# A bank of its own for the sums of r in a GRU with a mixture of experts behind it; shared banks for units and expert blocks

## The reference

```python
def cell(h, x):
    gi = x @ W_ih + b_ih
    gh = h @ W_hh + b_hh
    i_r, i_z, i_n = jnp.split(gi, 3, axis=-1)
    h_r, h_z, h_n = jnp.split(gh, 3, axis=-1)
    r = jax.nn.sigmoid(i_r + h_r)
    z = jax.nn.sigmoid(i_z + h_z)
    n = jnp.tanh(i_n + r * h_n)
    h_new = (1.0 - z) * n + z * h
    return (h_new, h_new)
...
gu = jnp.einsum('th,ehf->etf', x, w_gate_up)
act = _silu_and_mul(gu)
eo = jnp.einsum('eti,eih->eth', act, w_down)
routed = jnp.einsum('te,eth->th', combine, eo)
shared = _silu_and_mul(x @ w_sh_gate_up) @ w_sh_down
```

## Time and profile before

| | us |
|---|---|
| median of 3 runs | 1204.74 (1201.41 to 1206.31) |
| the profiled execution | 1195.19 |
| its span | 1193.4 |
| TensorE (PE) busy | 1036.9 (87%), 13452 products |
| VectorE (DVE) busy | 850.0 (71%) |
| ScalarE (ACT) busy | 573.3 (48%) |
| GpSimd (POOL) busy | 206.2 (17%) |

### The profile page before, as it was taken

One profiled execution on the slowest core, in us unless ns is written; L12 is line 12 of the kernel. 1 busy time (PEld: TensorE's weight loads), 2 busy tenths in 40 slices (PEclk: granted clock), 3 DMA queues, 4 the chain that ended last, 5 costly groups with the idle time before them and its releaser, 6 DMA issues.

```text
span 1193.4 us, 35909 instructions
## 1 busy us (share of the span) xinstructions
PE 1036.9 (87%) x13452; PEld 623.1 (52%) x13452; DVE 850.0 (71%) x4089; ACT 573.3 (48%) x1877; POOL 206.2 (17%) x213
## 2 busy tenths in 40 slices
PE   2789888889999898999899989998998898889894
PEld 2556555556665454555455545554555454555452
DVE  5898999868889888677867787678787778721111
ACT  4755555655555543445344434443444444435442
POOL 0200011020110212111211121112120112233332
PEclk9999999999999999999999999999999999999897
DMA  8943455381864753623451234234342144488694
GB/s 307 402 147 97 144 180 186 107 205 56 294 237 173 197 193 73 230 75 61 125 178 29 55 101 166 56 55 174 129 126 55 28 143 134 121 296 278 181 288 56
DMA packets 68829, 183.13 MB, mean 153 GB/s; under 512 B 7737, under 2 KB 40288, under 8 KB 61344
## 3 DMA queue, kind: packets, MB, share of 16 engines
q1 hardware_dynamic: 45632, 107.74, 25.5%
q0 software_dynamic: 23024, 73.11, 23.1%
HBM read 137.01 MB, written 52.87 MB: 159 GB/s over the span
## 4 chain that ended last, share of the span: by engine, by line
PE 51%; DVE 27%; ACT 10%; issue 7%; DMA 3%; POOL 0%; POOLq 0%; SPq 0%; ACTq 0%; DVEq 0%
PE psG L715 17%; PE psG L721 14%; PE psU L778 6%; DVE arena L1046 5%; DVE arena L1044 5%; ACT arena L1429 4%; ACT arena L1425 4%; PE psS L824 3%; DVE arena L1054 3%; DVE arena L1069 3%; DVE arena L1065 3%; DVE arena L1056 3%; PE psD L790 3%; DVE arena L1048 2%; PE psO L845 2%
## 5 line engine op out<-in xcount | busy, mean ns | idle before, releaser
L715 PE MATMUL psG<-arena 128*32 128x384 f16 x4096 | 213.8, 329 | 76.1 <-DVE arena L1069 68.2
L1425 ACT ACTIVATE arena<-arena 128x32 f32<-128x32 f32 x256 | 58.6, 229 | 336.7 <-DVE arena L1048 335.3
L721 PE MATMUL psG<-arena 128*32 128x384 f16 x4096 | 211.9, 327 | 3.7 <-issue 3.7
L778 PE MATMUL psU<-arena 128*128 128x256 f16 (+1 forms) x1920 | 203.7, 253 | 0.2 <-DVE arena L940 0.2
L1044 DVE STREAM_TRANSPOSE arena<-psG 128x128 f32<-128x128 f32 x256 | 81.1, 317 | 144.8 <-PE psG L721 138.2
L778 PEld LDWEIGHTS psU<-arena 128*128 128x128 f16 x1920 | 157.7, 99 | 49.1 <-issue 13.6
L715 PEld LDWEIGHTS psG<-arena 128*32 128x32 f16 x4096 | 86.2, 96 | 175.0 <-DVE arena L1069 141.9
L1625 POOL DMA_INDIRECT y<-arena x55 | 87.6, 1593 | 393.4 <-DVE arena L1046 312.2
L721 PEld LDWEIGHTS psG<-arena 128*32 128x32 f16 x4096 | 109.9, 97 | 60.9 <-issue 4.4
L1046 DVE STREAM_TRANSPOSE arena<-psG 128x256 f32<-128x256 f32 x256 | 104.1, 407 | 0.0
L790 PE MATMUL psD<-arena 128*128 128x512 f16 x384 | 97.6, 382 | 4.9 <-DVE arena L1264 4.9
(11 more groups left out here) (166 smaller groups left out, 1557.7 us busy)
## 6 DMA issues: line engine op xcount, KB each, us to landing
arena<-expert_weights SPq DMA_DIRECT2D x39, 1536.0 KB, 8.6
arena<-wgu POOLq DMA_DIRECT2D x32, 512.0 KB, 5.5
expert_weights<-arena POOLq DMA_DIRECT2D x9, 1536.0 KB, 6.8
gi_scratch<-arena SPq DMA_DIRECT2D x84, 128.0 KB, 2.0
arena<-gi_scratch SPq DMA_DIRECT2D x14, 768.0 KB, 5.6
arena<-wd POOLq DMA_DIRECT2D x16, 512.0 KB, 5.7
arena<-x SPq DMA_DIRECT2D x8, 512.0 KB, 4.0
hidden_rows<-arena SPq DMA_DIRECT2D x16, 256.0 KB
```

The lines of the kernel that those rows point to most:

```text
L715: e.matmul(psG[32 * j:32 * j + 32, 0:384], prev[:, c, 2:6].rearrange("p q n -> p (q n)"), whv[c][1][:, :, :, 32 * j:32 * j + 32], start=(c ...
L721: r = e.matmul(psG[32 * j:32 * j + 32, 0:384], prev[:, c, 0:4].rearrange("p q n -> p (q n)"), whv[c][0][:, :, :, 32 * j:32 * j + 32], star ...
L778: r = e.matmul(psU[u % 2][:, 256 * gu:256 * gu + width], half(W_GS + ex * 4 + c, pw)[:, o:o + 128], hh[:, 1 - ph, c, first:first + width], ...
L1425: e.activation(Ur, Ur, ACT.Tanh, scale=reg_tr).then_inc(th_r, 1)
```

## The change

1. The sums of r get a bank of their own (`psR`). The 32 products of a step become 64: with the low half of the weights 16 of 128 columns for r and 16 of 256 for z and n, then the same with the high half. The last one for r tells `step_r`, the last one of all `step_mm`.
2. On VectorE the transposition of r waits for `step_r`, the other for `step_mm`. The sum of r, which stood behind both before too, now also waits for `placed`.
3. `psU0` and `psU1` become one `psU`. Units and blocks share the banks `psU` and `psS`, behind the loop `psR` and `psG` too. The planner keeps count of them: a unit or block starts when one is free, and takes the first.
4. `s_gate` and `e_gate` go first among ScalarE's pieces of a step; `s_up` and `e_up` may stand in the same step as they.
5. `warm` sends products of 256 columns into `psG`, in steps with less than 1.0 us of pieces.

```diff
+    EARLY = ("s_gate", "e_gate")
...
+        if a[0] in self.EARLY:
+            return 0
+        if name[0] in self.EARLY and here == "DVE":
+            return 1
...
+        free, last, self.sums = {0: 0, 2: T, 3: T}, {}, {}
...
+                    sums = name[0] in ("s_unit", "up") and name[2] == 0
+                    ok = ok and not (sums and not any(f <= t for f in free.values()))
...
+                    if sums:
+                        i = min(free, key=lambda i: (free[i], i))
+                        del free[i]
+                        self.sums[name[:2]] = i, last.get(i)
+                        last[i] = name[:2]
+                    if name[0] in ("s_up", "e_up"):
+                        free[self.sums[("s_unit" if name[0] == "s_up" else "up", name[1])][0]] = t + 1
+                    if name == ("gates_out", 95):
+                        free[1] = t + 1
...
+        for names in self.at["ACT"].values():
+            names.sort(key=lambda n: n[0] not in self.EARLY)
...
-                before += [("s_up", u - 2)] if u > 1 else []
...
-            before += (chain("e_up") or [("gates_out", 95)]) if c == 0 else []
+            before += [("gates_out", 95)] if c == 0 else []
...
+        def sums_bank(name):
+            return (psU, psS, psR, psG)[PLAN.sums[name][0]]
...
-                for c in range(KC):
-                    for j in range(4):
-                        e.matmul(psG[32 * j:32 * j + 32, 0:384], prev[:, c, 2:6].rearrange("p q n -> p (q n)"),
-                                 whv[c][1][:, :, :, 32 * j:32 * j + 32], start=(c == 0), stop=False,
-                                 tile_position=(0, 32 * j))
+                def products(ps, gates, planes, part, first):
+                    n = 128 * len(gates)
+                    for c in range(KC):
+                        for j in range(4):
+                            ins = e.matmul(ps[32 * j:32 * j + 32, 0:n], prev[:, c, planes:planes + 4].rearrange("p q n -> p (q n)"),
+                                           whv[c][part][:, gates[0]:gates[-1] + 1, :, 32 * j:32 * j + 32],
+                                           start=(first and c == 0), stop=(not first and c == KC - 1), tile_position=(0, 32 * j))
+                    return ins
+
+                products(psR, (0,), 2, 1, True)
+                products(psG, (1, 2), 2, 1, True)
                 need(e, g_lo, t)
...
+                products(psR, (0,), 0, 0, False).then_inc(step_r, 1)
+                products(psG, (1, 2), 0, 0, False).then_inc(step_mm, 1)
...
-                if 2 < t < T - 1 and PLAN.load("PE", t) < 1.2:
-                    warm(t, int((1.45 - PLAN.load("PE", t)) / 0.165))
+                if 2 < t < T - 1 and PLAN.load("PE", t) < 1.0:
+                    warm(t, int((1.1 - PLAN.load("PE", t)) / 0.11))
```

More of the change, by code:

```diff
@@ L571, in wait_copied, with wait_sums @@
             e.wait_ge(bank_free, BANK[name] + 1)
+        def sums_bank(name):
+            return (psU, psS, psR, psG)[PLAN.sums[name][0]]
+        def wait_sums(e, name):
+            i, last = PLAN.sums[name]
+            if last is None and i == 0:
+                e.wait_ge(gi_ev_a, 6)
+                e.wait_ge(gi_ev_v, 6)
+            elif last is None and i == 1:
+                e.wait_ge(gi_ev_a, 12 * NBLK - 6)
+            elif last is None:
+                e.wait_ge(tr_r if i == 2 else tr_zn, T)
+            elif last[0] == "s_unit":
+                e.wait_ge(s_up, last[1] + 1)
+            else:
+                e.wait_ge(e_up, last[1] + 1)
         block = ctx.enter_context(nc.Block())
@@ L852, in warm @@
                 for _ in range(n):
-                    e.matmul(psG[:, 0:384], trih, whv[0][0][:, :, :, 0:32], start=True, stop=True)
+                    e.matmul(psG[:, 0:256], trih, whv[0][0][:, 1:3, :, 0:32], start=True, stop=True)
             spread_cross(1, PX0, 2)
```

53 lines of the change are left out of this document (21 added, 32 removed).

## The result

| | before | after |
|---|---|---|
| median | 1205.53 us (4 runs, 1201.41 to 1207.48) | 1217.53 us (4 runs, 1217.26 to 1218.22) |
| ratio | | 1.0105, 95% interval 1.0078 to 1.0132 |
| span of the profiled execution | 1193.4 | 1215.8 |
| loop, first to last step's start | 982.75 | 983.94 |
| behind the last step's start | 161.34 | 182.37 |

The forecast was 1175. The change made the kernel 12 us slower. Two views place the loss. First the windows, of the same stretches as the earlier trace rows: us, then busy time (instructions) of PE, PEld, DVE, ACT and POOL, TensorE's clock, DMA share and GB/s.

A forecast was written before the change was run, and what follows sets the result against it. The recurrence's chain of waits was taken to bound most steps, TensorE close behind. Chain -56, TensorE +16, VectorE +5, waits +2, tail +3 make -30 us, off the 1204.74 median: 1175 us, range 1157 to 1192.

The forecast's parts named there:

- Chain, 3.59 in light steps: Recurrent loop: transposing r before the other products end shortens a period from 3.81 to 3.59 us, 56 us in all.
- Spacing of short products, 0.057 and 0.109: Recurrent products on TensorE: groups of four start 0.057 us (128 columns) and 0.109 us (256 columns) apart.
- The rival that short groups are fed too slowly: Recurrent products: 128-column groups take 0.10 us, not 0.057, adding 0.35 us per step; about 1260 us, chance 0.04.
- TensorE takes back 16 us: Loop: 99 steps with over 2.06 us of placed TensorE work run longer than the new chain, 16 us in sum.
- VectorE and new waits, forecast at 7 us: Loop: VectorE's placed work delays transpositions, 5 us; waits added by gates going first on ScalarE, 2 us.
- The single stalls are left as they are: Loop: the single stalls, 11 us over the typical periods, the longest 3.69, were taken as unchanged.
- supply of instructions is the bound: Rival, TensorE's loop: 80 products per step at 0.071 us each make 5.7 us a step, some 1680 us; chance 0.03.
- the 62 ns for every MATMUL: TensorE's sequencer, quoted from the Trainium skill for hardware decoding off: about 62 ns per product, an estimated 4.96 us a step.
- Tail +3 (-8 to +10): Behind the loop: leftover products, block pairs and waits together add 3 us, between -8 and +10.
- The 4.6 us of products left over: Tail: two more units and the second half of block 20 are left to it, 4.6 us of products.
- Some 1 us of waits where now 0.7 a block: Tail: blocks go in pairs, the second's gate products following its transposition without filler; some 1 us of waits.
- 915.5 + 16 + 5 + 2: Loop without stalls: periods at 3.59 us, plus 16 for TensorE, 5 for VectorE and 2 for added waits.

The follow-up runs named there:

- e3: The changed kernel with the recurrence's products undivided in psG as before, planner and banks as changed: 1219.69 us, 1.0175 of the kernel before.
- e7: The changed kernel with the products split only in the 142 steps with under 2.3 us of placed TensorE work: 1200.08 us, 1.005 of the kernel before.
- e4: The changed kernel with the planner's old rules behind step 255 (gates later, first up product waits for e_up): 1209.68 us, 1.0087 of the kernel before.
- e8: The changed kernel with the edits of e4 and e7, and its 512 KB copies cut into four: 1185.05 us, 0.990 of the kernel before.
- e17: The changed kernel with the edits of e4 and e7, copies uncut, on another chip: 1188.10 us, 0.9915 of the kernel before.
- e13: The kernel before with 64 long-satisfied waits added on TensorE's queue behind each step's recurrent products: 2996.53 us.

## Why the prediction was wrong

- **Chain, 3.59 in light steps: nearly.** Measured 3.63. L1079 starts 0.44 behind L1077 (the last products are done only then) and takes 444 ns for L1046's 407; the sum of r stands 0.37 behind it where 0.33 was taken.
- **Spacing of short products, 0.057 and 0.109: right.** The last product of a step starts 1.23 us in (forecast 1.22) and the transposition of r at 1.12 (1.11). The rival that short groups are fed too slowly fell.
- **TensorE takes back 16 us: right.** 51 x 0.02 + 62 x 0.20 = 13 us. VectorE and new waits, forecast at 7 us, are inside the 3 us that all remaining steps lie over their typical periods, but for one step (at 246.6, below).
- **"The single stalls are left as they are": this sentence failed.** They went from 11 to 44 us (here a step is named by the start of its L1077). 26.5 us (before 4.7) lie in the 17 steps with a gap at the end of a block, with the slower products behind it: the clock was 0.80 from 259 to 270 us, behind the 6.04 us stall. In one of the 17 (at 408.6) VectorE also stood 2.66 us for something that the trace calls remote, so the late blocks' own part is some 24 us. 14.1 us (before 3.2) lie in 11 other steps, most in three: at 596.3 TensorE waited 2.99 us for gathered rows, in front of the next recurrence; in the step at 236.3 VectorE stood 2.64 us for something remote, and TensorE 1.14 us for nothing the trace shows. In the third, at 246.6, ScalarE stood 1.10 us and then loaded an activation table in front of its first gate, and VectorE's half of that gate, which may now stand in the same step, held up the transposition of r (ScalarE, then VectorE):

```profile
249.86 1.28 ACT L1511 ACT_TABLE_LOAD   x1 [1.10 <-remote]
...
251.58 0.48 DVE L1292 SCALAR_TENSOR_TENSOR arena<-arena,psU 128x256 f32<-128x256 f32 x1 [2.18 <-ACT arena L1511]
```

  The kernel before loads the same table at 251.7 us, and there nothing on VectorE waits for it in that step.
- **The rival "supply of instructions is the bound" had the right resource and the wrong form.** It was priced as a rate (0.071 us a product, 1680 us, chance 0.03), and the rate was never short: a step with seven chunks has 85 products in 3.83 us, 0.045 us each. That also speaks against the 62 ns for every MATMUL that the prediction quotes there. It says that its trace does not contradict them, but the 24 products in 0.76 us of the earlier trace rows already did. What was short is the time in which one block of 256 has to be fetched. The earlier trace rows showed one such stall of 3.69 us; I read it and gave it no mechanism. Its place in the order (193 modulo 256, the sequencer's waits counted) and the 106 packets on the page would have given one.
- **Tail +3 (-8 to +10): mis-sized, +21.** The 4.6 us of products left over were right (3.9). "Some 1 us of waits where now 0.7 a block" was not: the copies out of psT cost 25 us for 2.6, since `down` and the turned activations waited too, which I hadn't priced. e3 shows that the planner and banks alone make it.
- **The sum.** Without stalls and tail the forecast holds: 939 us of steps where 938.5 was taken (915.5 + 16 + 5 + 2). That it holds so closely is luck: the chain took 11 us more than forecast (255 x 0.04), TensorE's share was 3 less, and the 7 for VectorE and waits don't show in the typical periods. The error is 33 us of stalls and 18 us of tail: -30 + 51 = +21, and the two profiled executions differ by 22 (1195.19, 1217.61). The medians differ by 12 only, since the median before lies 10 us over its profiled execution and the one after does not.

## What to carry to other kernels

Count an edit's instructions as well as its work: if an engine takes 256 of them in less time than a fetch can need under full DMA (here about 6 us: 4 until the packet starts and 2.2 from there), each such block may stop it, and the "issue" stalls of the trace of before, numbered modulo 256, show how near that is. Put the longer instruction stream only where it shortens something: split in the light steps alone, the loop was 19 us shorter than before (e7), and with the tail of e4 the kernel was 1% faster (e8, e17). When a planner's rules change for the loop, price its order behind the loop by who waits for whom, not by the number of pieces.

## What the runs showed of the hardware that was not expected

- TensorE's instructions come in packets of 16 KB (256). With the DMA engines 86% busy or more the next one started up to 10.7 us behind the end of the block ahead, and no block started less than 2.18 us behind its packet. The gaps at the ends of blocks in the loop, ordinary waits that fall there included: 6 to 7 us at 106 or 107 packets, 4 at 126, 10 to 12 at 142, 14 to 22 at 170 or 171, 75 at 234.
- On two of the four chips of the experiments TensorE stops for 0.5 to 0.7 us at the end of an indirect DMA's issue on GpSimd, 11 to 26 times in the kernels with split products and not in those without; on the others it doesn't. The same change was 1.0105 of the kernel before in its first runs and 1.020 on one of these two chips.
- Waits that were long satisfied followed one another at 0.106 us (median) on TensorE's sequencer when 64 stood in a row (e13).
